# The first tile's third gate and up chunk computed ahead of the seam between attention and feed-forward

## What is computed

```
x = x + cross_attention(layernorm(x), ctx, ctx; Wq, Wk, Wv, Wo and their biases)   # 16 heads of 32
x = x + ffn(layernorm(x))

ffn(x):   gate = fp4_linear(x, w_gate); y = fp4_linear(x, w_up)     # 512 -> 1408
          h = silu(gate) * y
          return fp4_linear(h, w_down)                              # 1408 -> 512
fp4_linear(x, w) = quant_dequant(x) @ quant_dequant(w).T            # blocks of 16 along the last axis
```

## Time and profile before

| | |
|---|---|
| median of 3 runs | 2138.82 us (2137.6 to 2141.08) |
| the profiled execution | 2137.12 us |
| its span in the trace | 2135.3 us |
| TensorE busy | 2070.8 us (97%) |
| VectorE busy | 1708.5 us (80%) |
| ScalarE busy | 863.6 us (40%) |
| mean granted clock of TensorE | 0.987 |

### The profile page before, as it was taken

How to read it: one execution, slowest core, us unless ns; L and a number is a source line. 1 busy time by engine, 2 the same in 40 slices (tenths; PEclk the granted TensorE clock), 3 DMA queues, 4 the chain that set the end, 5 groups by cost and what they waited for, 6 DMA issues and landing times. The chain is left out here.

```text
span 2135.3 us, 42263 instructions
## 1 busy us (share of the span) xinstructions
PE 2070.8 (97%) x16730; PEld 1785.7 (84%) x16730; DVE 1708.5 (80%) x2859; ACT 863.6 (40%) x1753; POOL 144.7 (7%) x162
## 2 busy tenths in 40 slices
PE   6999999999999999999999999978899999999998
PEld 5888888888988888888888898856688888888886
DVE  6777777777777777777768777777999999999985
ACT  5555455455554555555545455453111111111111
POOL 0000000000000000000000000001101001001000
PEclk9999999999999999999999999979899999999999
DMA  4443444534445344344553545454343343344331
GB/s 162 119 137 98 130 110 135 140 97 132 109 133 139 101 126 139 100 137 109 132 139 95 132 109 134 111 151 129 107 133 109 113 137 112 114 131 113 114 113 38
DMA packets 159462, 257.36 MB, mean 121 GB/s; under 512 B 34096, under 2 KB 102704, under 8 KB 156832
## 3 DMA queue, kind: packets, MB, share of 16 engines
q1 hardware_dynamic: 158544, 253.34, 43.1%
q10 hardware_dynamic: 720, 1.31, 0.2%
HBM read 109.88 MB, written 57.54 MB: 78 GB/s over the span
## 5 line engine op out<-in xcount | busy, mean ns | idle before, releaser
L756 DVE TENSOR_REDUCE row_max<-gate_bank 128x1 f32<-128x376 f32 (+1 forms) x576 | 301.8, 536 | 114.6 <-PE gate_bank L565 113.6
L539 PE MATMUL proj_bank<-attention_operands 128*128 128x256 f32 x2304 | 304.8, 282 | 0.0
L517 PE MATMUL proj_bank<-attention_operands 128*128 128x376 f32 (+1 forms) x1536 | 288.8, 337 | 3.6 <-ACT attention_operands L690 3.1
L539 PEld LDWEIGHTS proj_bank<-attention_operands 128*128 128x128 f32 x2304 | 288.8, 189 | 0.4 <-DVE q_part L786 0.2
L654 ACT ACTIVATE probs<-score_bank 125x448 f32<-125x448 f32 x384 | 208.0, 542 | 163.5 <-PE score_bank L579 161.1
L517 PEld LDWEIGHTS proj_bank<-attention_operands 128*128 128x128 f32 x1536 | 262.1, 190 | 5.9 <-issue 3.4
L1402 ACT ACTIVATE f_act_gate<-gate_bank 128x512 f32<-128x512 f32 (+1 forms) x84 | 47.3, 564 | 528.4 <-PE up_bank L1342 528.4
L654 ACT ACTIVATE probs<-up_bank 125x448 f32<-125x448 f32 x384 | 208.0, 542 | 126.7 <-PE up_bank L579 124.2
L1342 PE MATMUL gate_bank<-gate_up,early 128*128 128x512 f32 (+1 forms) x984 | 226.7, 380 | 17.2 <-DVE early L1484 9.3
L1342 PEld LDWEIGHTS gate_bank<-gate_up,early 128*128 128x128 f32 x984 | 183.7, 191 | 50.2 <-DVE early L1484 9.6
L1342 PE MATMUL up_bank<-gate_up,early 128*128 128x512 f32 (+1 forms) x984 | 223.8, 376 | 0.0
(11 more groups left out here) (146 smaller groups left out, 3194.5 us busy)
## 6 DMA issues: line engine op xcount, KB each, us to landing
kstack<-k_low SPq DMA_DIRECT2D x256, 93.8 KB, 2.3
kstack<-early SPq DMA_DIRECT2D x256, 93.8 KB, 2.2
kstack<-k_high SPq DMA_DIRECT2D x256, 93.8 KB, 2.2
strips_scratch<-f_strips SPq DMA_DIRECT2D x25, 960.0 KB, 3.7
f_turned<-strips_scratch SPq DMA_DIRECT2D x100, 240.0 KB, 4.4
ctx_raw<-in_ctx SPq DMA_DIRECT2D x15, 1500.0 KB, 8.0
qstack<-early SPq DMA_DIRECT2D x384, 28.0 KB, 1.9
qstack<-q_part SPq DMA_DIRECT2D x384, 28.0 KB, 1.8
```

The costliest lines, as they stand in the source:

```text
L517: last = nc.tensor.matmul(out[:, 0:hi - lo], w_hi_lo[W_K][ws][:, c, g * P:(g + 1) * P], ctx_part[cs][:, c, lo:hi], start=(n == 0), stop=(n ...
L539: last = nc.tensor.matmul(out[:, 0:256], ctx_part[cs][:, c, kt * KW:kt * KW + P], w_hi_lo[W_V][ws][:, c, half * 256:(half + 1) * 256], sta ...
L756: nc.vector.tensor_reduce(row_max[:, m, kh:kh + 1], mbank[:, 0:KSPLIT[kh + 1] - KSPLIT[kh]], AX.X, ALU.max).then_inc(max_reduced, 1)
```

## The change

The products of chunk 2 of the first tile (24 matmuls of 128x384) leave the feed-forward block and stand as `first_gate` 2 behind `first_gate` 1, ahead of the seam. They need two more PSUM banks that are kept over it: `first_banks` grows from four to six, and the new two are the feed-forward's `turn_bank0` and `turn_bank1`. In the attention these serve as the second score bank and as `pv_bank`, so `first_gate` 2 also waits until the last heads are normalized out of `pv_bank`. Its wait for split weight tiles is for all 22 of them. In the feed-forward, the SiLU and `hidden` of (0, 2) read the two turn banks, TensorE skips all of tile 0's `gate_up`, and `gate_up` (1, 1) (q = 4) waits for the first `hidden` alone, since chunk 2 no longer went through its bank pair.

```diff
--- before.py
+++ after.py
@@ -299,7 +299,7 @@
 LAST_UNITS = last_units()
 END_UNITS = [unit for place, unit in sorted(attend_units(NG - 1), key=lambda item: item[0]) if place >= 12]
 END_UNITS += [("ffn_store", 2), ("inverse", 3, 0), ("inverse", 3, 1), ("heads", 3), ("heads_hi", 3), ("sum_lo", 3), *end_tiles(16, 20), ("first_gate", 0), ("out", 0, 0), *end_tiles(20, 22), ("out", 0, 1)]
-END_UNITS += [("store_x1", 0, 0), ("store_x1", 0, 1), ("first_gate", 1), ("ffn_regroup", 2)]
+END_UNITS += [("store_x1", 0, 0), ("store_x1", 0, 1), ("first_gate", 1), ("first_gate", 2), ("ffn_regroup", 2)]
 
 
 def attention(nc, ctx, dram, ident, ln_consts, x1, ffn_raw, ffn_quant, ffn_squares, batches, region, ctx_raw, early, gate_up, xqt, first_banks, fs):
@@ -379,9 +379,9 @@
     shift_rows = [q[:, :, :].rearrange("p h q -> p (h q)").rearrange("p (m c) -> p m c", c=P) for q in qstack]
 
     max_bank = first_banks[0:3]
-    score_bank = [first_banks[3], bank("score_bank1")]
+    score_bank = [first_banks[3], first_banks[4]]
     proj_bank = [bank(f"proj_bank{i}") for i in range(2)]
-    pv_bank = bank("pv_bank")
+    pv_bank = first_banks[5]
 
 
     names = ("score", "max", "shift", "k", "q", "v", "xt", "out", "pv")
@@ -605,17 +605,18 @@
                     pe.wait_ge(w_lo_done, SPLIT_ORDER.index(t) + 1)
                 elif kind == "first_gate":
                     pe.wait_ge(fs["x_lo"], 1)
-                    pe.wait_ge(turn_lo, 8 * (t + 1))
+                    pe.wait_ge(turn_lo, min(8 * (t + 1), EARLY_TILES))
                     if t == 0:
                         pe.wait_ge(max_reduced, 2 * MT * NG * batches)
                         pe.wait_ge(shift_copied, NG * batches)
                     else:
                         pe.wait_ge(exp_done, 12 * NG * batches)
+                        pe.wait_ge(normalized, NG * batches)
                     for m in range(2):
                         n = 0
                         for c in range(KC):
                             for xs_, ws in PASSES:
-                                last = nc.tensor.matmul(first_banks[2 * t + m][:, :], xqt[0][xs_][:, c, :],
+                                last = nc.tensor.matmul(first_banks[2 * t + m][:, 0:CH[t + 1] - CH[t]], xqt[0][xs_][:, c, :],
                                                         gate_up[m][ws][:, c, CH[t]:CH[t + 1]], start=(n == 0), stop=(n == 11))
                                 n += 1
                     last.then_inc(fs["gated"], 1)
@@ -1196,9 +1197,9 @@
     rstd = sb("f_rstd", [P, 1])
     spacer = sb("f_spacer", [P, 1])
 
-    gate_bank = first_banks[0::2]
-    up_bank = first_banks[1::2]
-    turn_bank = [bank(f"turn_bank{i}") for i in range(2)]
+    gate_bank = [first_banks[0], first_banks[2]]
+    up_bank = [first_banks[1], first_banks[3]]
+    turn_bank = [first_banks[4], first_banks[5]]
     down_bank = [bank(f"down_bank{i}") for i in range(2)]
 
     x_loaded = fs["x_loaded"]
@@ -1328,13 +1329,13 @@
         def body(i, units):
             for kind, n, *rest in units:
                 tile = 2 * i + n
-                if kind == "gate_up" and (tile > 0 or rest[0] == 2):
+                if kind == "gate_up" and tile > 0:
                     c = rest[0]
                     q = 3 * tile + c
                     par = (3 * n + c) % 2
                     w = CH[c + 1] - CH[c]
                     reached(pe, x_lo, tile + 1)
-                    reached(pe, hidden_done, q - 1)
+                    reached(pe, hidden_done, 1 if q == 4 else q - 1)
                     for m, banks in ((0, gate_bank), (1, up_bank)):
                         k = 0
                         for kc in range(KC):
@@ -1399,7 +1400,8 @@
                     w = CH[c + 1] - CH[c]
                     act.wait_ge(gated, q + 1)
                     reached(act, hidden_done, q - 1)
-                    nc.scalar.activation(act_gate[par][:, 0:w], gate_bank[par][:, 0:w],
+                    gate = turn_bank[0] if q == 2 else gate_bank[par]
+                    nc.scalar.activation(act_gate[par][:, 0:w], gate[:, 0:w],
                                          ACT.Silu).then_inc(silu_done, 1)
                 elif kind == "turn_h":
                     c = rest[0]
@@ -1494,7 +1496,8 @@
                     dve.wait_ge(silu_done, 3 * tile + c + 1)
                     if c == 0 and tile > 0:
                         dve.wait_ge(q_steps, quant_count(tile + 2, 4))
-                    nc.vector.tensor_tensor(hidden[:, chunk(c)], act_gate[par][:, 0:w], up_bank[par][:, 0:w],
+                    up = turn_bank[1] if tile == 0 and c == 2 else up_bank[par]
+                    nc.vector.tensor_tensor(hidden[:, chunk(c)], act_gate[par][:, 0:w], up[:, 0:w],
                                             ALU.mult).then_inc(hidden_done, 1)
                 elif kind == "turn_h_lo":
                     c = rest[0]
@@ -1538,7 +1541,7 @@
             return whole.enter_context(nc.semaphore(name))
 
         first_banks = [whole.enter_context(nc.psum_tensor(n, [P, 512], F32))
-                       for n in ("gate_bank0", "up_bank0", "gate_bank1", "up_bank1")]
+                       for n in ("gate_bank0", "up_bank0", "gate_bank1", "up_bank1", "turn_bank0", "turn_bank1")]
         fs = {n: sem(f"f_{n}") for n in ("gated", "ln_steps", "pow_steps", "x_normed", "q_steps", "x_turned", "x_hi", "x_lo",
                                          "x1_stored")}
         fs["x_loaded"] = [sem(f"f_x_loaded{i}") for i in range(2)]
```

## The result

The changed kernel takes 2142.24 us, the median of 22 runs (2139.75 to 2146.74), against 2139.69 us for the kernel before, also of 22 runs (2136.72 to 2142.97). The ratio is 1.0014, 95% interval 1.0007 to 1.0020, so +3.0 us (1.5 to 4.3): a small loss, within the 0.2% that the prediction set as its bound. The time stands in the range, 0.8 us under the 2143.0 that was predicted. All ratios are of fast runs; one run of the kernel before, of 4081.39 us, in the comparison that E5 to E8 share, is left out of them.

The account below looks back on a forecast made before the run. The prediction took TensorE as last at the seam, then VectorE's chain to the first `down`, then TensorE, as the bound. 4.19 - 0.1 = +4.1 us on the profiled execution gave 2141.2, against the median 2142.9, stated 2143.0; range 2138.5 to 2146.5.

Parts of the forecast that it names:

- The seam moves by 4.19 us: At the barrier, TensorE arrives last, so the 24 added matmuls delay it from 1462.3 to 1466.5 us.
- The removal gives nothing: Behind the seam, dropping TensorE's 24 matmuls (6.99 us) gives VectorE's chain 0 us.
- (b): Distance from the first load behind the seam to the first `down`; forecast to stay at 59.4 us.
- rival of TensorE leading the start-up: Behind the seam, VectorE would wait through SiLUs for TensorE, so removal pays: -4.4 us, 2134.4 us; chance 0.05.
- Loads land sooner, 0.1 us: Behind the seam, with SyncE's regroup further along, loads could give back 0 to 0.9 us; 0.1 taken.
- VectorE starts with x, not with it: Behind the seam, VectorE's chain starts with x, not the 4.48 us load, limiting what a sooner load gives back.
- absorbed case: At the seam, another engine holds it or loads give back over 2 us: about 2140 us; chance 0.12.
- TensorE's pauses behind the seam: After `gate_up` (1, 1), ending near 1488.7 us, TensorE idles 3.7 us instead of 1.64 until `hidden` (1, 0).
- The 1.82 us at the first `down` stay in both: The first 33 `down` matmuls lose 1.82 us to the low clock, before and after alike.
- everything from `hidden` (1, 0) on keeps its distances: From `hidden` (1, 0) to the first `down`, timing is unchanged, the reason given for the same 1.82 us clock cost.
- the clock takes more: Longer pauses behind the seam keep TensorE at 1.2 GHz into (2, 0) to (2, 2) and `down`: +7.3 us, 2146; chance 0.08.
- the clock takes less: At the first `down`, no low-clock stretch: +2.3 us, 2141.1 us; chance 0.03.

Follow-up runs that it names:

- E5: The kernel before, with 8 matmuls of 128x384 put into TensorE's pause ahead of the first `down`; ratio 0.9991 (0.9983 to 1.0000).
- E8: The changed kernel again, unchanged, for a second profile and more runs; ratio 1.0015 (1.0006 to 1.0024) to the kernel before.
- E3: The changed kernel with the 24 matmuls ahead of the seam made twice; ratio 1.0035 (1.0023 to 1.0047) to the kernel before.
- E4: The kernel before, with the second chunk's up product (12 matmuls of 128x512) moved behind the seam; ratio 0.9990 (0.9981 to 0.9999).
- E6: The kernel before, with the whole second chunk behind the seam and the last regroup ahead of the two x1 stores; ratio 0.9988 (0.9979 to 0.9997).
- E2: The changed kernel with the 24 matmuls also made behind the seam, and those results used; ratio 1.0025 (1.0015 to 1.0035) to the kernel before.
- E1: The changed kernel without `first_gate` 2, so the third chunk's products are never made; ratio 0.9995 (0.9986 to 1.0004) to the kernel before.
- E12: The changed kernel once more, unchanged, for a third profile; ratio 1.0018 (1.0009 to 1.0027) to the kernel before.
- E10: The kernel before, unchanged, against itself: a second profile and null comparison; ratio 1.0004 (0.9995 to 1.0013).
- E9: The changed kernel with 8 matmuls of 128x384 filling the pause ahead of the first `down`; ratio 1.0020 (1.0011 to 1.0028) to the kernel before.
- E7: E6 plus the third tile's x loaded ahead of the seam and `hidden` (0, 0) behind quant step 6; ratio 0.9971 (0.9960 to 0.9981) to the kernel before.
- E11: E7 with 8 matmuls filling the pause ahead of the first `down`; 2130.95 us against 2138.56 for the kernel before, ratio 0.9964.

## Why the prediction was right, and where it was not

*The seam moves by 4.19 us.* Right: +4.16, +4.17 and +4.16 in the three profiles of the changed kernel, and twice that in E3. TensorE held the seam, and E4 and E6 show the cover: where SyncE is last, it holds it.

*The removal gives nothing.* Right: distance (b) is the same with the work and without it (E2 and the changed kernel 59.46 and 59.37), and E1 alone gains no measurable time. The rival of TensorE leading the start-up is excluded: it would have made (b) shorter by 7 to 8.6 us.

*Loads land sooner, 0.1 us.* From the first load's issue to VectorE's first instruction it was 2.71, 2.65 and 2.72 us in the changed kernel's three profiles, 2.81 and 2.82 in the two of before. The x came 0.1 us sooner, but (b) didn't shrink by it (59.37 against 59.38), because in the profiles of before and of the changed kernel the chain that ended last ran through the first down weights instead: 4.48 us of load in the kernel before and 4.46 us, from 1467.84, in the changed one, each followed by 0.64 us of ScalarE's split. So "VectorE starts with x, not with it" was right for VectorE's start and not for the chain. Where this load leads (before, the changed kernel, E8, E12, E2, E3, E4), (b) is 59.37 to 59.83 us; where x leads (E10, E1, E9, E5), it is 58.96 to 59.17, which would account for E1's 0.2 us. (E6, with its late x, has 59.73.) A give-back of over 2 us, the absorbed case, is excluded. That SyncE's regroup "is not delayed" was wrong: its four issues took 1.1 us longer, which TensorE's drain hid.

*TensorE's pauses behind the seam.* The forecast put `gate_up` (1, 1) at 1488.7 and a pause of 3.7 us behind it; it ended at 1487.24, and the pause was 5.17. The forecast had priced more of (1, 0) at the low clock than there was: its gate product took 4.42 us and its up product 2.96. In this longer pause the clock fell, and (1, 2) ran its first 12 matmuls in 4.18 us, where they took 2.32 before. That is what the Trainium skill (TensorE: Matmul & The Clock Gate, the part on HAM oscillation) has pauses between bursts do, and the trace agrees. It was hidden, as worked out: the SiLU was done 6 us ahead of `hidden` (1, 2).

*The 1.82 us at the first `down` stay in both.* This is the step that failed: "everything from `hidden` (1, 0) on keeps its distances" holds for VectorE and not for the clock. The start of (2, 0) keeps its distance to the first `down`, 19.75 us. But in the changed kernel (2, 0) runs longer at 1.2 GHz, 8.18 us from its first gate matmul to the start of (2, 1) where it was 7.05. TensorE is done 1.1 us later, the pause ahead of `down` shrinks from 2.76 to 1.65 us, and the clock doesn't fall in it. The 33 matmuls then take 7.80 us instead of 9.35. The size was off too: 1.82 us compared 9.52 with 7.70, but 33 matmuls at full clock behind a pause are printed as 7.96, and from start to start the low clock costs 1.55 us. The rival "the clock takes more" had the cause, more of (2, 0) at the low clock, and expected the opposite of it: at this size the delay only used up TensorE's room, and with it the pause.

So the loss is 4.16 - 1.55 and some 0.1 elsewhere, 2.7 us, and the measured 3.0 (1.5 to 4.3). The ratios of E8, E12 and E9 lie above it by 0.5 to 1.6 us, which is of the size that the null comparison E10 shows. The case "the clock takes less", +2.3 us, had been given 0.03; it was in fact the case in every profile of the changed kernel. That 2143.0 is only 0.8 us off is partly luck. The rise of 4.2 us was too large (the medians differ by 2.55), and the median of before that it started from, 2138.82 of 3 runs, was 0.9 us under the one of 22.

E5 and E9 show the cause from both sides: filling the pause removes the low stretch where there is one and brings nothing where there is none. In all fourteen profiles pauses up to 1.77 us went with 7.8 us, and pauses from 2.29 us on with 9.3.

Why the clock returned later in (2, 0) stays open. The slices in which it returned, in the kernel before, the changed one and E4, and E4's (2, 0):

```profile
1504.99:1505.19 0.20, 0.20 (x2) 0.16 (x2) 0.20 (x1) 0.00 (x0) 0.00 (x0) 0.95 0.00 0
1511.49:1511.69 0.20, 0.20 (x2) 0.19 (x1) 0.20 (x1) 0.00 (x0) 0.00 (x0) 0.74 1.19 259
1507.50:1507.70 0.20, 0.20 (x2) 0.10 (x2) 0.17 (x2) 0.00 (x0) 0.00 (x0) 0.67 0.00 0
```

```profile
1503.62 4.87 PE L1343 MATMUL gate_bank<-gate_up,early 128*128 128x512 f32 x12 [7.71 <-DVE early L1485]
```

From the start of (2, 0) to the clock's return it is 3.0 to 3.3 us in the kernel before, E10, E1, E5, E6, E7 and E11, 4.0 and 4.1 in E4 and E3, and 5.2 to 5.7 in the changed kernel, E8, E12, E9 and E2. The later it comes, the later TensorE is done and the shorter is the pause (2.76, 2.33 and 1.65 us in the kernel before, E4 and the changed kernel). So it goes with the addition and not with the removal (E2 has it, E1 hasn't), and E3 has it in part. E4 hints at what it hangs on: counted from `first_gate` 0 the clock returns there at 59.4 us, and at 59.7 to 59.9 in the kernel before, E10, E1 and E5, although (2, 0) starts at 55.4 us in E4 and at 56.5 to 56.9 in those. The moment didn't follow the work that had moved. No run singles out what sets it.

## What to carry to other kernels

At a full barrier ask first which engine's drain ends last, and count every piece of work moved ahead of the barrier at its full price if it is on that engine, even where the engine is the busiest of the kernel; what it frees behind the barrier is worth nothing if another engine leads there. Here the right direction was the opposite: take work off the last arriver until the next one holds the barrier, then move that one's work, then move the first load behind the barrier ahead of it (E4, E6, E7: 1.5, 4.0 and 7.4 us by the profiles, a and b together; 2.1, 2.6 and 6.2 us by the ratios). A short pause on the chain is worth filling with work whose result is dropped, if the clock falls in it (E5, E11: 1.5 us).

## What the runs showed of the hardware

The clock's last rise ahead of the first `down`, and the fall at it, repeated for each kernel. In the two profiles of before it rose 42.6 and 42.5 us behind the first load of the seam and fell at 59.7 and 59.6; in the three of the changed kernel it rose at 45.1, 44.9 and 44.9 and had no fall near 59. This although `first_gate` 0 started 2.76 us apart in the two, and up to 2.76 us apart in the three. The Trainium skill (same page, part 1), which the prediction cited for transitions that vary from run to run, is borne out only for earlier moments (the first fall behind the seam came at 1.7 and at 5.0 us in the two profiles of before, and in E12 one fall at 38.1 us where its two sisters had it at 34.9 and 34.7). On the chain it isn't: in these two and three profiles the pause (within 0.12 us) and the price at the first `down` were the same each time, so the change in clock behaviour there is most likely the change's and not chance.

The start of `first_gate` 0 was 1445.11 and 1447.87 us in two profiles of the same kernel, and 1444.87 to 1450.32 in all fourteen. That spread, made in the attention, is as large as the effects measured here. Spans of single executions can't be compared at this size; distances from a common mark can.
